# Attention without gate: parts of the row maxima as rows of the Q stack, in place of selection matmuls

## The reference

```python
q = (x @ wq + wq_b); k = (y @ wk + wk_b); v = (y @ wv + wv_b)     # y: x itself, or 77 rows of context in Y
logits = einsum('bhqd,bhkd->bhqk', q, k) / sqrt(8)
attn = softmax(logits, axis=-1)
out = einsum('bhqk,bhkd->bhqd', attn, v)
x = layernorm(x + out @ wo + wo_b)
```

## Time and profile before

| | us |
|---|---|
| median of 3 runs | 5442.49 (5440.62 to 5445.76) |
| profiled execution | 5428.83, of which span 5427.1 |
| TensorE busy | 4056.8 (75%), 29692 matmuls |
| VectorE busy | 4319.6 (80%) |
| ScalarE busy | 2781.0 (51%) |
| GpSimd busy | 3163.7 (58%) |
| mean granted clock of TensorE | 0.865 of full |

### The profile page before, as it was taken

One profiled execution on the slowest core, in us unless ns is written; L12 is line 12 of the kernel. 1 busy time (PEld: TensorE's weight loads), 2 busy tenths in 40 slices (PEclk: granted clock), 3 DMA queues, 4 the chain that ended last, 5 costly groups with the idle time before them and its releaser, 6 DMA issues. The chain is left out here.

```text
span 5427.1 us, 104523 instructions
## 1 busy us (share of the span) xinstructions
PE 4056.8 (75%) x29692; PEld 2331.6 (43%) x29692; DVE 4319.6 (80%) x8453; ACT 2781.0 (51%) x6469; POOL 3163.7 (58%) x3426
## 2 busy tenths in 40 slices
PE   5878778887787778874888678883747788688843
PEld 2333333333333333332666456652735666466611
DVE  5999999999999999994888767763356777666678
ACT  4555555555555555552777534434654445344434
POOL 5888888878888888874777533326452222333302
PEclk8998999889989989986999889995877888799955
DMA  2111111111110111102655366544125555465511
GB/s 84 67 49 54 69 68 68 42 62 69 68 69 33 69 68 68 69 37 46 105 102 102 60 119 110 104 88 151 57 89 107 95 96 95 82 112 102 98 39 31
DMA packets 320209, 420.99 MB, mean 78 GB/s; under 512 B 40000, under 2 KB 301712, under 8 KB 309136
## 3 DMA queue, kind: packets, MB, share of 16 engines
q1 hardware_dynamic: 315536, 408.35, 32.3%
q0 software_dynamic: 4352, 8.95, 0.5%
HBM read 307.65 MB, written 109.58 MB: 77 GB/s over the span
## 5 line engine op out<-in xcount | busy, mean ns | idle before, releaser
L2202 POOL TENSOR_TENSOR m_h<-m_dtu,m_Bb 128x512 f32<-128x512 f32 x1024 | 1598.1, 1590 | 148.4 <-PE bank L1835 146.1
L1835 PE MATMUL bank<-m_h,ident 128*128 128x512 f32 x2048 | 1245.2, 699 | 404.5 <-DVE m_h L2101 398.8
L1835 PEld LDWEIGHTS bank<-m_h,ident 128*128 128x128 f32 x2048 | 370.6, 210 | 1083.8 <-DVE m_h L2101 931.3
L2095 DVE TENSOR_TENSOR_SCAN m_h<-m_dA,m_h 128x512 f32<-128x512 f32 x512 | 771.0, 1506 | 0.5
L2101 DVE TENSOR_TENSOR m_h<-m_h,bank 128x512 f32<-128x512 f32 x1024 | 672.1, 656 | 14.4 <-PE bank L1828 14.4
L2095 DVE TENSOR_TENSOR_SCAN m_h<-bank,m_h 128x512 f32<-128x512 f32 x512 | 620.4, 1212 | 16.5 <-ACT bank L1983 9.5
L1983 ACT ACTIVATE bank<-m_dt,m_A 128x512 f32<-128x512 f32 x512 | 352.5, 688 | 378.6 <-DVE m_h L2095 273.6
L1983 ACT ACTIVATE m_dA<-m_dt,m_A 128x512 f32<-128x512 f32 x512 | 366.9, 717 | 350.1 <-DVE m_h L2095 343.4
L688 DVE TENSOR_REDUCE x_nm<-bank 128x4 f32<-128x308 f32 x512 | 242.7, 474 | 184.0 <-PE bank L359 181.1
L531 ACT ACTIVATE x_sm<-bank,x_nm 128x77 f32<-128x77 f32 x1024 | 318.2, 336 | 62.5 <-DVE x_nm L688 62.1
L688 DVE TENSOR_REDUCE f_nm<-bank 128x4 f32<-128x512 f32 x256 | 175.7, 687 | 120.2 <-PE bank L359 119.1
(11 more groups left out here) (425 smaller groups left out, 10366.2 us busy)
## 6 DMA issues: line engine op xcount, KB each, us to landing
m_Bb<-m_B SPq DMA_DIRECT2D x32, 4096.0 KB, 12.2
x_Ks<-x_k_parts SPq DMA_DIRECT2D x32, 462.0 KB
x_q_parts<-x_qp SPq DMA_DIRECT2D x32, 384.0 KB, 4.0
x_Qs<-x_q_parts SPq DMA_DIRECT2D x32, 384.0 KB
f_Ks<-f_k_parts SPq DMA_DIRECT2D x16, 768.0 KB
a_Ks<-a_k_parts SPq DMA_DIRECT2D x16, 768.0 KB
x_xp<-x_stage SPq DMA_DIRECT2D x32, 256.0 KB
x_Qs<-x_q_parts SPq DMA_DIRECT2D x32, 256.0 KB
```

What stands on the lines that cost most here:

```text
L1835: pe.matmul(banks[4 + c], ident[:], h[:, k % RING, :], start=(s == 0), stop=(s == NS - 1)).then_inc(s_ya.sem, 1)
L2095: v.tensor_tensor_scan(h[:, k % RING, :], decays[k % AHEAD], h[:, k % RING, :], 0.0, ALU.mult, ALU.add).then_inc(s_h.sem, 1)
L2202: pool.tensor_tensor(h[:, k % RING, :], dtu[:, d, c, :], Bb[:, d, s, :], ALU.mult).then_inc(s_dB.sem, 1)
```

## The change

- The constant sel goes. In its place is pick, 128 rows x 16 heads, with a one in row 64 + 16 x part + head.
- At the start of a stage without gate ScalarE writes rows 64 to 127 of Ks: pick, repeated over all keys (two copies, one for each half of the double buffer). VectorE clears rows 0 to 63 of Ks alone. nmT is no longer cleared.
- maxima_rows now writes rows 64 to 111 of nmT. From there the rows of a sequence are copied into rows 64 to 111 of the Q stack, 16 heads wide: chunks 0 and 1 by ScalarE (two copies of 48 x 512), chunks 2 and 3 by VectorE (one copy of 48 x 1024).
- So the matmul of the transposed scores, over all 128 rows, adds the maxima itself, and the selection matmul goes. The row scores use rows 0 to 63 of the stacks (in x0, with gate, still all).
- The shifted scores and their exponentials come one chunk later in the order: chunks 0 and 1 of sequence b - 1 at chunks 2 and 3 of step b, chunks 2 and 3 at chunks 0 and 1 of step b + 1. ScalarE's copies stand at chunks 0 and 1 behind its other work of the step, VectorE's at chunk 1 behind the maximum and norm. shifted waits for these copies; maxima_rows waits for ScalarE's copies of the sequence before.

```diff
+            return (1, c - T_AT) if c >= T_AT else (2, c - T_AT + 4)
...
+            return (Qs[PICK:PICK + PARTS * H, lb // GB, 4 * lo:4 * hi, q * S:(q + 1) * S],
+                    nmT[PICK:PICK + PARTS * H, lb % 2, :].unsqueeze(1).to_broadcast([PARTS * H, 4 * (hi - lo), S]))
...
+                rows = P if gate is not None else HALF
...
+                    ins = pe.matmul(bankS[c % 2][:, h * sk:(h + 1) * sk], Qs[0:rows, l, hh, q * S:(q + 1) * S],
+                                    Ks[0:rows, l, hh, q * sk:(q + 1) * sk], start=(mask is None), stop=(mask is None or h == 3))
...
-                pe.wait_ge(s_nmT.sem, s_nmT.at(b + 1))
+                if c < BY_ACT:
+                    pe.wait_ge(s_ma.sem, s_ma.at(b, c + 1))
+                else:
+                    pe.wait_ge(s_md.sem, s_md.at(b + 1))
...
-                    pe.matmul(o, Ks[:, l, hh, q * sk:(q + 1) * sk], Qs[:, l, hh, q * S:(q + 1) * S],
-                              start=True, stop=False)
-                    ins = pe.matmul(o, sel[:, hh, 0:sk], nmT[:, lb % 2, :], start=False, stop=True)
+                    ins = pe.matmul(o, Ks[:, l, hh, q * sk:(q + 1) * sk], Qs[:, l, hh, q * S:(q + 1) * S],
+                                    start=True, stop=True)
...
+            if gate is None:
+                for l in range(2):
+                    act.activation(Ks[HALF:P, l], pick[HALF:P, :].unsqueeze(2).to_broadcast([HALF, H, kt]), ACT.Copy).then_inc(s_zero.sem, 1)
...
+            def lay_rows(b, lm, c):
+
+                act.wait_ge(s_nmT.sem, s_nmT.at(b + 1))
+                act.activation(*max_rows(lm, c, c + 1), ACT.Copy).then_inc(s_ma.sem, 1)
...
-                v.wait_ge(s_st.sem, s_st.at(b - 1))
-                v.tensor_copy(nmT[0:PARTS * H, lm % 2, :], bankMb[0:PARTS * H, 0:S]).then_inc(s_nmT.sem, 1)
+                v.wait_ge(s_ma.sem, s_ma.at(b - 1))
+                v.tensor_copy(nmT[PICK:PICK + PARTS * H, lm % 2, :], bankMb[0:PARTS * H, 0:S]).then_inc(s_nmT.sem, 1)
+
+            def lay_rows(v, ch, b, lm):
+                v.wait_ge(s_nmT.sem, s_nmT.at(b + 1))
+                v.tensor_copy(*max_rows(lm, BY_ACT, 4)).then_inc(s_md.sem, 1)
...
-            pool.memset(sel[:], 0.0).then_inc(s, 1)
+            pool.memset(pick[:], 0.0).then_inc(s, 1)
...
-                pool.affine_select(out=sel[:], in_=sel[:], compare_op=ALU.not_equal, fill=1.0, base=-part * H,
-                                   pattern=[[-1, H], [0, P]], channel_multiplier=1).then_inc(s, 1)
+                pool.affine_select(out=pick[:], in_=pick[:], compare_op=ALU.not_equal, fill=1.0, base=-P // 2 - part * H,
+                                   pattern=[[-1, H]], channel_multiplier=1).then_inc(s, 1)
```

More of the change, by code:

```diff
@@ L83, in attention @@
     K_TIMES = (3, 2, 1)
+    HALF, PICK = P // 2, P // 2
+    T_AT = 2
+    BY_ACT = 2
     VC, VT = 16, 32
@@ L87, in attention @@
     TAIL = 6
-    ident, identb, ones_row, sel = const["ident"], const["identb"], const["ones_row"], const["sel"]
+    ident, identb, pick = const["ident"], const["identb"], const["pick"]
     half_pow = const["half_pow"]
@@ L174, in attention @@
         s_S = sem("scores", 4); s_Sf = sem("scores_used", 4); s_nmp = sem("max_parts"); s_T = sem("max_transposed")
-        s_nmT = sem("max_rows"); s_st = sem("shifted", 4); s_e = sem("exp", 4)
+        s_nmT = sem("max_rows"); s_ma = sem("max_rows_laid_by_act", BY_ACT); s_md = sem("max_rows_laid_by_dve"); s_st = sem("shifted", 4); s_e = sem("exp", 4)
         s_gp = [sem(f"gate_loaded{l}", 16) for l in range(2)]; s_tw = sem("weights_turned", 4); s_ev = sem("weights_copied", 4)
@@ L187, in attention @@
         bankMb = bankM.bitcast(BF16)
-        NZ = 2 + (gate is None) + (sk < P)
+        NZ = 2 + 2 * (gate is None) + (sk < P)
         NW = sum(1 for t in (bq, bk, bv, bo) if t is not None) + 4 + (2 if ln is not None else 0) + (2 if rms else 0)
@@ L431, in step @@
                         turn_weights(b - 1, (lb - 1) % 8, c)
[L432 to L435, removed]
+                else:
+                    k, chunk = turned_chunk(c)
+                    if live(k):
+                        shifted(b - k, (lb - k) % 8, chunk)
+                    if c == 0 and live(1):
                         turn_max(b - 1, (lb - 1) % 8)
-                elif live(1):
-                    shifted(b - 1, (lb - 1) % 8, c - 1)
                 if live(2):
@@ L546, in step @@
                 else:
[L547 to L550, removed]
+                    k, chunk = turned_chunk(c)
+                    if live(k):
+                        exp(b - k, (lb - k) % 8, chunk)
                 if c == 0 and live(4):
@@ L554, in step @@
                     act.activation(oT[:], bankY[:, 0:S], ACT.Copy).then_inc(s_oT.sem, 1)
+                if c < BY_ACT and live(1) and gate is None:
+                    lay_rows(b - 1, (lb - 1) % 8, c)
             def slots(i, lb, c, last):
@@ L587, in _ @@
         def _(dve):
-            dve.memset(Ks[:], 0.0).then_inc(s_zero.sem, 1)
-            if gate is None:
-                dve.memset(nmT[:], 0.0).then_inc(s_zero.sem, 1)
+            dve.memset(Ks[0:P if gate is not None else HALF], 0.0).then_inc(s_zero.sem, 1)
             if sk < P:
@@ L763, in step @@
                     norm(v, ch, b - 5, (lb - 5) % 8)
+                if c == 1 and live(1) and gate is None:
+                    lay_rows(v, ch, b - 1, (lb - 1) % 8)
                 if c == 2 and live(3):
@@ L2631, in constants @@
     ones_row = st.enter_context(nc.sbuf_tensor("ones_row", [1, P], F32))
-    sel = st.enter_context(nc.sbuf_tensor("sel", [P, H, P], BF16))
+    pick = st.enter_context(nc.sbuf_tensor("pick", [P, H], BF16))
     half_pow = st.enter_context(nc.sbuf_tensor("half_pow", [P, 4 * GB], F32))
@@ L2648, in _ @@
             for part in range(3):
-                pool.affine_select(out=sel[:], in_=sel[:], compare_op=ALU.not_equal, fill=1.0, base=-part * H,
-                                   pattern=[[-1, H], [0, P]], channel_multiplier=1).then_inc(s, 1)
+                pool.affine_select(out=pick[:], in_=pick[:], compare_op=ALU.not_equal, fill=1.0, base=-P // 2 - part * H,
+                                   pattern=[[-1, H]], channel_multiplier=1).then_inc(s, 1)
                 pool.wait_ge(s, 8 + part)
-    return {"ident": ident, "identb": identb, "ones_row": ones_row, "sel": sel, "half_pow": half_pow}
+    return {"ident": ident, "identb": identb, "ones_row": ones_row, "pick": pick, "half_pow": half_pow}
 def build(nc, a, out, stages="MXFNYQ"):
```

5 lines of the change are left out of this document (3 added, 2 removed).

## The result

The changed kernel takes 5483.37 us, median of five runs (5470.59 to 5496.74), against 5442.49 for the kernel before (five runs, 5434.42 to 5452.83): 1.0075 times the time of before, interval 1.0056 to 1.0094. So it is slower, by 41 us. The forecast was 5377 us, faster, with a range of 5320 to 5440; the result lies outside.

The account below looks back on a forecast made before the run. TensorE and VectorE were taken to wait for each other, neither full. Sequences -67, a1's start +9 and constants -8 gave -66 us: 5428.8 to 5363 for the profiled execution, 5377 as median; range 5320 to 5440.

Parts of the forecast that it names:

- Row scores over 64 rows: TensorE's row scores: moving columns unchanged, cost taken 0; one form change per chunk at most 24 us a stage.
- (a): Rival on TensorE: less work leaves more gaps, the granted clock falls, about 30 us of gain lost, 5407 us; chance 0.14.
- (b): Rival on TensorE: the array form change costs 24 us in x1, 12 each in f0 and a1, 5425 us; chance 0.10.
- its last part: Signs to check; copy over 0.85 us, clock lower by 0.05 or row-to-shifted score spacing over 0.1 us would refute it.
- (c): Rival on TensorE: waits for the row of maxima go with no successor, +32 and +15 us gain, 5330 us; chance 0.12.
- (d): Rival on VectorE: its copy is long, at 1.3 us adding 154 us, four fifths exposed, 5497 us; chance 0.13.
- (e): Rival on ScalarE: its two copies delay exponentials and squares; a1, f0 gain nothing, x1 half, 5432 us; chance 0.08.
- Selection matmuls: TensorE: 16 matmuls a sequence removed, 0.87 us a sequence, 56 us a stage, ceiling 167 us, not reached.
- The order: TensorE: waits for the row of maxima leave as shifted starts at chunk 2; 0.3 us a sequence in x1.
- Copies: Each sequence: VectorE's one copy at 0.5 us; ScalarE's two at some 0.6 each, hidden in idle time, cost 0.
- Starts: Stage starts: ScalarE's one-hot rows delay a1 by 9 us, x1 and f0 by 0; shorter constants save 7.6 us.
- The sum: Whole kernel: -67 from the sequences, +9 from a1's start, -8 from the constants, -66 us in all.

Follow-up runs that it names:

- e2: Changed kernel with row scores over all 128 rows, exponentials scaled by 1/64, maxima stale, so not the reference's result: 5361.9 us, ratio 0.9863.
- e1: Kernel before with only the row scores of the stages without gate reading 64 rows instead of 128: 5565.0 us, ratio 1.0241.
- the loops: Kernel before with seven TensorE-only matmul loops ahead of its first stage, mixing 64-row, 128-row and 32-column forms: 0.446 us for eight alike, 0.656 for four and four.
- loops 3 and 5: Ahead of the kernel before, from idle: 40 chunks of four (loop 3) or eight (loop 5) 64-row, four 128-row, four 32-column matmuls: 66.4 and 83.5 us.
- e10b: Changed kernel with 128-row row scores (maxima stale, exponentials scaled by 1/64) and every shifted score issued twice: 5400.5 us, ratio 0.9928.
- e6: Kernel before with only the new order, shifted scores and exponentials one chunk later, selection matmuls kept: 5360.9 us, ratio 0.9855.
- e9b: Changed kernel with 128-row row scores (maxima stale, exponentials scaled by 1/64) and the old order of shifted scores: 5561.3 us, ratio 1.0214.

## Why the prediction was wrong, step by step

- **Row scores over 64 rows, cost taken 0: the step that failed.** It is worth 121.5 us (changed kernel less e2; 128 in e1), and the forecast bounded it at 24 us a stage from the one form change that it saw. The size of a drain was right: 0.095 from the earlier trace rows, 0.105 in the loops. At x1's end, at full clock in e1 and in before, it is all there is: a sequence takes 6.19 us in e1 instead of 5.86, 0.08 a chunk, which is 21 us a stage. Over the whole of x1 e1 loses 49 us, and its clock goes from 0.95 to 0.91. What was missing is the clock: chunks of this form alone, after a stop, stay at the lower level (loops 3 and 5, and f0's end), where those of 128 rows leave it. The size can be estimated. Time at the lower level is 2 x (1 - clock) x length, which for the spread of f0 gives 2 x 0.24 x 558 = 268 us in the changed kernel and 2 x 0.14 x 491 = 137 in e2; half of the 131 us between them is lost work, 66 us, against the 67 us that f0 is longer. In a1 it is 298 less 139, so 80 us of lost work and 39 on the time; in x1 58 less 48, 5 us, of 16. Together that is 151 us of lost work for 123 us of time: the right size, but no exact account, since in f0 it leaves nothing for the drains and in a1 it is twice what the time shows.
- **Rivals (a) and (b)** were named apart and priced at 30 and 48 us. The result is (b)'s cause through (a)'s effect; what (a) named, fewer matmuls, did take f0 from 0.92 (e10b) to 0.86 (e2), but the total stayed near the forecast. The text had the warning in its last part, a clock lower by 0.05 and a spacing of over 0.1 us, but no case joined them. (c) came, hidden under the rest: it said that the waits for the row go with no successor, and priced that at 47 us; e6 shows 80. (d) and (e) didn't come.
- **Selection matmuls.** Ceiling 167 us, taken as nearly the whole gain. They are worth 39. At f0's end, where 5.0 us a sequence was forecast, the last four of e2 take 5.39, 5.09, 6.03 and 5.08, in the mean 5.40 against 5.42 before; at a1's end a sequence went from 6.12 to 6.00, where 5.8 was, while the order alone brings it to 5.38.
- **The order.** One half sentence of the forecast, "the waits for the row of maxima leave TensorE too", was worth 80 us; the forecast took 0.3 us a sequence for it in x1, on TensorE's side, where VectorE's was the longer one, and nothing in a1. The row that said so stood in the earlier trace rows.
- **Copies.** VectorE's were forecast at 0.5 us and take 0.44 to 0.55; ScalarE's at 0.6, and take 0.63 at a cost taken 0. Together with the starts they cost 40 us, on a term of the sum that had them only on VectorE's side and inside the net gains.
- **Starts.** ScalarE's one-hot rows: 14 us forecast and 13.9 measured in a1, 8.5 and 8.5 in x1. In a1 the first evacuation stands right behind them and the first turn_max comes 57.9 us after the block's first instruction instead of 50.1: 8 us for 9. The constants end 7.1 us earlier (3.84 + 6.30 in the earlier trace rows, now 2.13 + 0.87) for 7.6:

```profile
2.13 0.87 POOL L2678 TENSOR_SCALAR_AFFINE_SELECT pick<-pick 128x16 bf16<-128x16 bf16 x3
```

- **The sum** of -66 us is -76 in the kernel without the form (e2, 0.9863). It was near by luck: order -80, matmuls -39, copies and starts +40, and then the form +121.5. That these add to +42.5, near the measured +41, is no proof of them, since each is the difference of neighbours in one chain of runs. In another sequence the parts would be priced otherwise, as e9b shows.

## What to carry to other kernels

A matmul over fewer rows costs as many cycles and is not free: give it the full rows if zeros can stand there, and look at the granted clock of a stretch with TensorE busy throughout, not at the busy time, to see whether it is being paid for. Before a change with several parts is built, try the one that only moves work: here the order was worth more than all else, at no instruction. And where a chain waits, price the wait by its row first; the matmuls taken off beside it were worth a quarter of their time.

## What the runs showed of the hardware

- After a stop of some 24 us, chunks of 4 x 64-row, 4 x 128-row and 4 fp32 matmuls into 32 columns stayed at a granted clock of 0.50 for all of 66 us with TensorE busy throughout; with 128 rows in all of them it was 0.95 over 38 us. The same chunks that began at 1.00 stayed at 1.00 for 161 us. So what a pattern is granted depends on what it starts from. Of two chunks with the same matmuls and the same changes of form, the one with 4 x 64 and 8 x 128 rows was at 0.96 over 51 us, the one with 8 x 64 and 4 x 128 rows at 0.50 over 83.5 us.
- More work can bring the clock back: 1024 further 128-row matmuls in f0 took its spread from 558.8 to 530.1 us, at a clock of 0.88 instead of 0.76.
- A change between 64-row and 128-row matmuls costs 0.105 us at full clock; the row count alone changes nothing in the spacing (0.446 us for eight of either).
- A GpSimd clearing of 48 x 2048 bf16 (1.80 us) stretched VectorE's copy of 48 x 1024 bf16 from a mean of 522 to 1195 ns, and its operation of 128 x 4 fp32 from 171 to 1279 ns (in f0; in a1 the copy went from 435 to 459 only).
